# A recommendation tower: gathered groups turned by VectorE out of one table, 16-bit ids, single waits for pairs of tiles, and the first layer in parts

## The chip, the cores and the metric

One core of a Trainium2 chip runs the whole kernel in one launch. The time is device microseconds of that core, a median over several executions. The core has TensorE (PE, matrix products into PSUM), VectorE (DVE), ScalarE (ACT), GpSimd (POOL, here used to issue gathers) and SyncE (SP, here used to issue the direct DMAs). A kernel's engines run their own instruction lists in order, and meet at semaphores.

## The reference

```python
# ids (512, 40) int32; tbl_f (1000 to 125000 rows, 32) float32
e = jnp.stack([tbl_0[ids[:, 0]], ..., tbl_39[ids[:, 39]]], axis=1)     # (512, 40, 32)
iidx, jidx = jnp.triu_indices(40, k=1)                                 # 780 pairs
z = jnp.einsum('bpd,pde,bpe->bp', e[:, iidx], bilinear_matrices, e[:, jidx])
h = jnp.concatenate([z, dense_ctx], axis=1)                            # (512, 796)
h = jnp.maximum(h @ W_top1 + b_top1, 0.0)                              # (512, 512)
h = jnp.maximum(h @ W_top2 + b_top2, 0.0)                              # (512, 256)
y = h @ W_top3                                                         # (512, 1)
```

For each of 780 pairs of fields, one embedding row is multiplied by a 32x32 matrix and then by the other field's row, for each of the 512 samples; the 780 numbers and 16 dense inputs go through three layers.

## The kernel before, in words

**Groups.** The 40 fields form 10 groups of 4. A group's embeddings stand in `xt[:, t, :]` as 128 rows (4 fields times 32) by 512 samples, in float32. There are two ways to fill a group.

- Four groups (positions 0, 1, 3 and 5, `HOT_POS`) hold small tables and are picked by matrix product. VectorE compares the ids of the group, broadcast to all partitions, with a row number ("hot" steps, L320), and TensorE multiplies the 0/1 result by the table in three bfloat16 pieces (L385). The pieces `rest` and `low` come from VectorE too (L330, L332). 8, 8, 10 and 10 such rounds make 36 rounds. Ids are int32; ScalarE turns them to float16 (`narrow_ids`, L271), and all rounds but the first two compare the float16 ids.
- Six groups (`GATHER_POS`) are gathered row by row by 96 indirect DMAs that GpSimd issues (L217), 16 a group, each of 128 rows of one field's table. TensorE transposes four 128x128 tiles into `t_ps` (a "turn" step, L396), and ScalarE copies them to `xt` (L289).

**Units.** A unit (t, u), u up to t, covers all pairs of groups t and u; there are 55, in the order (0,0), (1,0), (1,1), (2,0) and so on. For each of the 4 fields of u (3 where u = t, called a diagonal unit here) TensorE makes one tile of `y_ps` with a 32-row matmul (L423); the trace shows two instructions per matmul. VectorE multiplies pairs of tiles by `xt[:, t, :]` into `prod` (L345, two instructions a unit, half 2k and half 2k+1 for unit k), and TensorE adds up over the 32 embedding rows with a selecting matrix into `z_ps` (a "sum" step, L446). Every 8 units ScalarE copies `z_ps` to a block of `z_t` (L294). There are 7 blocks.

**Buffers.** `y_ps` has 3 slots of 2 banks, so a half uses the slot of the half three before it. Before unit k TensorE waits once, for half 2k-2 to be read, which is more than its first pair of tiles needs. `z_ps` and `t_ps` have a bank each; `t_ps` is shared by rounds, turns and first-layer steps.

**Order.** It is written by hand: `schedule()` makes one list for TensorE and ScalarE: unit k, sum k-1, then whatever `AFTER` puts behind unit k. `vector_schedule()` makes VectorE's list: the rounds of `AFTER` come ahead of the unit of that number. Of the 36 rounds 11 come ahead of unit 0 and 5 around it, the rest are spread up to unit 13.

**Layers.** The first layer takes 4 parts of 128 outputs by 7 blocks. Blocks 0 to 3 are four steps of 4 matmuls, after units 34, 36, 38 and 42 (L405). Blocks 4 and 5 come at the end, after sums 53 and 54 (`late_blocks`, L369), block 6 after that (L454), VectorE adds the two halves (L351), and then layer two (L460) and three (L469) follow.

**Loads.** SP issues in order: ids, broadcast ids and table of pick group 0, of 1, matrices, tables of 2 and 3, more matrices, dense inputs; then the ids of groups 2 and 3, each behind a wait for earlier rounds; then the remaining matrices and weights. ScalarE's queue issues the row numbers, the identity (`eye`) and the selecting matrix.

Of the kernel before, what the change touches and what calls it, by code (L numbers as in the profile page):

```python
# [9 lines left out]
F16 = mybir.dt.float16  # L10
# [22 lines left out]

HOT_POS = [0, 1, 3, 5]
# [4 lines left out]
GATHER_POS = [t for t in range(GROUPS) if t not in HOT_POS]  # L39

# [42 lines left out]
def schedule():  # L83
# [3 lines left out]
    for k in range(-1, UNITS + LAG):  # L87
# [7 lines left out]
        for what in ("turn", "hot", "l1"):  # L95
            steps += [(what, n) for n, after in enumerate(AFTER[what]) if after == k]
# [13 lines left out]
def fills_bank(what, k):  # L110

    return what in ("turn", "l1") or (what == "hot" and ROUND[k][1] == HOT_ROWS[ROUND[k][0]] - 1)


def bass_dlrm_tower(nc, ids, hot_ids, numbers, hot_tables, tables, dense, mats, w1, b1, w2, b2, w3, ident, select, dense_sel, out):
    steps = schedule()
    fills = [s for s in steps if fills_bank(*s)]

    def fills_to(what, k):

        return fills.index((what, k)) + 1
# [422 lines left out]
```

## Time and profile before

| | us |
|---|---|
| median of 3 runs | 220.88 (219.36 to 221.36) |
| the profiled execution | 218.29 |
| its span, first to last instruction | 216.5 |
| TensorE busy | 182.4 |
| VectorE busy | 162.2 |
| GpSimd busy | 98.1 |
| ScalarE busy | 25.7 |
| granted TensorE clock, mean | 0.997 of full |

The span is from the first to the last instruction of the profiled execution; its own time is 1.8 us more. Busy times of engines overlap, so they don't add up to the span; matmuls are pipelined, and their ends are modelled, so the distance between the starts of two things is a safer measure than the length of one. In the chain of waits each line is a piece of the one path that ended last.

### The profile page before, as it was taken

Reading aid. Unit: us, or ns where it says so; the run is one execution under the profiler, and the core shown is the slowest. Engines: PE = TensorE matmul, PEld = TensorE weight load, DVE = VectorE, ACT = ScalarE, POOL = GpSimd, SP = SyncE. Lnnn points to the kernel's source line nnn. Section 1 sums busy time; section 2 is a strip of 40 time slices with the busy share of each in tenths; the row PEclk is TensorE's granted clock in tenths of the full one; section 3 lists DMA queues with packets and bytes.
Section 4 is the critical chain, followed back from the end, with each engine's and each line's share of the span. In section 5 each row is a group of like instructions: output and inputs, shape, how many; then the busy total and the mean of one; then the engine's idle time right before and its main releaser. Section 6 shows DMA issues by size and latency. Waiting matters only on the chain.

```text
span 216.5 us, 3263 instructions
## 1 busy us (share of the span) xinstructions
PE 182.4 (84%) x1392; PEld 55.0 (25%) x1392; DVE 162.2 (75%) x158; ACT 25.7 (12%) x33; POOL 98.1 (45%) x100
## 2 busy tenths in 40 slices
PE   0097694998599998899988899999998899999993
PEld 0032121332133221221212222322222121233433
DVE  0699869998999989989989993473957898960500
ACT  2331223002010021010100101011201010001411
POOL 4787777777877777777777770000000000000000
PEclk9999999999999999999999999999999999999998
DMA  6998079920000100100010000000000000000000
GB/s 227 372 401 283 12 292 421 402 58 12 12 15 11 16 12 12 17 13 12 14 16 12 14 13 3 5 0 0 3 0 0 0 3 0 0 3 0 0 0 0
DMA packets 7950, 14.55 MB, mean 67 GB/s; under 512 B 2784, under 2 KB 6000, under 8 KB 7296
## 3 DMA queue, kind: packets, MB, share of 16 engines
q1 hardware_dynamic: 4432, 12.65, 15.2%
q0 software_dynamic: 3072, 1.58, 4.3%
q8 instruction: 11, 0.18, 0.3%
q10 hardware_dynamic: 432, 0.12, 0.2%
q14 instruction: 3, 0.02, 0.0%
HBM read 14.33 MB, written 0.00 MB: 66 GB/s over the span
## 4 chain that ended last, share of the span: by engine, by line
PE 54%; DVE 32%; issue 7%; DMA 3%; ACT 1%; SPq 0%; DVEq 0%
DVE prod L345 26%; PE y_ps L423 23%; PE z_ps L446 7%; PE t_ps L385 7%; PE t_ps L405 7%; PE y_ps L369 3%; DVE hot L320 3%; PE y_ps L460 3%; DMA table<-hot_tables 3%; DVE rest L330 2%; PE y_ps L454 2%; DVE low L332 1%; PE t_ps L396 1%; PE t_ps L469 1%; ACT xt L289 1%
## 5 line engine op out<-in xcount | busy, mean ns | idle before, releaser
L345 DVE TENSOR_TENSOR prod<-y_ps,xt 128x1024 f32<-128x1024 f32 x110 | 124.1, 1170 | 26.6 <-PE y_ps L423 19.3
L217 POOL DMA_INDIRECT x_rows<-tbl,ids_sb x96 | 97.9, 1019 | 31.6 <-issue 29.0
L423 PE MATMUL y_ps<-xt,m_sb 32*128 32x512 f32 x420 | 62.6, 639 | 11.0 <-DVE prod L345 10.8
L446 PE MATMUL z_ps<-prod,sel 128*32 128x512 f32 x420 | 58.5, 604 | 0.2
L385 PE MATMUL t_ps<-hot,table 128*32 128x512 bf16 x144 | 15.9, 403 | 19.2 <-DVE low L332 17.3
L320 DVE TENSOR_SCALAR hot<-hot_id,number 128x2048 bf16<-128x2048 f16 (+1 forms) x36 | 26.8, 788 | 6.2 <-DMA hot_id<-hot_ids 6.2
L423 PEld LDWEIGHTS y_ps<-xt,m_sb 32*128 32x128 f32 x420 | 17.5, 183 | 49.8 <-DVE prod L345 32.1
L446 PEld LDWEIGHTS z_ps<-prod,sel 128*32 128x32 f32 x420 | 8.7, 107 | 43.6 <-DVE prod L345 34.0
L385 PE MATMUL t_ps<-hot,low 128*32 128x512 bf16 x144 | 15.6, 393 | 0.0
L385 PE MATMUL t_ps<-hot,rest 128*32 128x512 bf16 x144 | 15.6, 393 | 0.0
L405 PE MATMUL t_ps<-z_t,w_sb 128*128 128x512 f32 x32 | 14.8, 605 | 0.0
L289 ACT ACTIVATE xt<-t_ps 128x512 f32<-128x512 f32 x10 | 6.0, 595 | 69.4 <-PE t_ps L385 39.9
L385 PEld LDWEIGHTS t_ps<-hot,table 128*32 128x32 bf16 x144 | 4.3, 96 | 31.3 <-DVE low L332 19.6
L294 ACT ACTIVATE z_t<-z_ps 128x512 f32<-128x512 f32 x7 | 4.2, 597 | 62.2 <-PE z_ps L446 62.2
L351 DVE TENSOR_TENSOR hot_id<-y_ps,hot_id 128x512 f32<-128x512 f32 x4 | 2.8, 692 | 8.8 <-PE y_ps L454 8.8
L271 ACT ACTIVATE hot_id<-hot_id 128x2048 f16<-128x2048 int32 x4 | 7.6, 1910 | 11.7 <-DMA hot_id<-hot_ids 11.7
L405 PEld LDWEIGHTS t_ps<-z_t,w_sb 128*128 128x128 f32 x32 | 5.7, 189 | 9.1 <-issue 9.1
L369 PE MATMUL y_ps<-z_t,w_sb 128*128 128x512 f32 x16 | 7.4, 606 | 0.0
L460 PE MATMUL y_ps<-hot_id,w_sb 128*128 128x512 f32 x16 | 7.0, 592 | 0.0
L286 ACT ACTIVATE hot_id<-t_ps,b_sb 128x512 f32<-128x512 f32 x4 | 2.7, 687 | 30.6 <-PE t_ps L405 30.6
L330 DVE TENSOR_TENSOR rest<-table 128x1024 f32<-128x1024 f32 (+1 forms) x4 | 5.4, 1350 | 1.0 <-DMA table<-hot_tables 1.0
L332 DVE TENSOR_TENSOR low<-rest 128x1024 bf16<-128x1024 f32 (+1 forms) x4 | 5.4, 1358 | 0.1
(20 smaller groups left out, 37.2 us busy)
## 6 DMA issues: line engine op xcount, KB each, us to landing
hot_id<-hot_ids SPq DMA_DIRECT2D x4, 1024.0 KB, 4.9
w_sb<-w SPq DMA_DIRECT2D x1, 1792.0 KB, 13.9
x_rows<-tbl,ids_sb POOLq DMA_INDIRECT x96, 2.4
table<-hot_tables SPq DMA_DIRECT2D x2, 640.0 KB, 10.5
table<-hot_tables SPq DMA_DIRECT2D x2, 512.0 KB, 6.8
m_sb<-mats SPq DMA_DIRECT2D x1, 640.0 KB, 9.0
m_sb<-mats SPq DMA_DIRECT2D x1, 576.0 KB, 7.7
m_sb<-mats SPq DMA_DIRECT2D x1, 512.0 KB, 6.8
```

What stands on the lines that cost most here:

```text
L217: pool.indirect_dma_start(out=x_rows[:, g, bt, f, :], out_offset=None, in_=tables[field], in_offset=row).then_inc(gathered[g], 16)
L271: nc.scalar.activation(hot_id16[:, o % ID_RING, :], hot_id[:, o % ID_RING, :], ACT.Copy).then_inc(hot_id16_done, 1)
L289: nc.scalar.activation(xt[:, t, :], t_ps[:], ACT.Copy).then_inc(t_out, 1)
L320: nc.vector.tensor_scalar(hot[:, k % HOT_RING, :, :].rearrange("p f b -> p (f b)"), ids_of[:, o % ID_RING, :], number[:, o, r:r + 1], None ...
L330: nc.vector.tensor_tensor(left, whole, upper(whole), ALU.subtract).then_inc(rest_done, 1)
L345: nc.vector.tensor_tensor(prod[:, k % PROD_UNITS, 2 * half:2 * half + w, :], y_ps[:, 2 * slot:2 * slot + w, :], xt[:, t, :].unsqueeze(1).t ...
L369: nc.tensor.matmul(y_ps[:, LATE_BANK[m], :], w1_sb[:, b, m * P:(m + 1) * P], z_t[:, b, :], start=(b == EARLY_BLOCKS), stop=False, skip_gro ...
L385: last = nc.tensor.matmul(t_ps[f * DIM:(f + 1) * DIM, :], pieces[piece][:, f, :], hot[:, k % HOT_RING, f, :], start=(r == 0 and piece == 0 ...
L405: last = nc.tensor.matmul(t_ps[:], w1_sb[:, b, m * P:(m + 1) * P], z_t[:, b, :], start=(b == 0), stop=(b == EARLY_BLOCKS - 1))
L423: last = nc.tensor.matmul(y_ps[:, 2 * slot + s % 2, :], m_sb[rows, k, :], xt[rows, u, :], start=True, stop=True)
L446: last = nc.tensor.matmul(z_ps[s * DIM:(s + 1) * DIM, :], window, prod[:, k % PROD_UNITS, s, :], start=starts, stop=(k >= last_unit(b) - 1 ...
L460: last = nc.tensor.matmul(y_ps[:, L2_BANK[c], :], w2_sb[:, m, c * P:(c + 1) * P], h1[:, m, :], start=(m == 0), stop=(m == M1 - 1), skip_gr ...
```

## The change

- Gathered groups: the host puts all tables of gathered fields into one array `rows` and gives, beside the ids, the first row of each field's table. GpSimd adds the two (one instruction), and gathers 32 samples of 4 fields at a time (partition 32s+i is field s, sample i of the chunk), again 96 indirect DMAs of 128 rows. VectorE transposes the group in 32x32 blocks straight into `xt` (`nc.vector.transpose`, 128x512), ahead of the first unit of the group. TensorE's transposes, the identity and ScalarE's copies for these groups are gone.
- Ids for comparing are the lower 16-bit halves (int16), for all four groups with a place of their own, so that SP waits for nothing and ScalarE converts nothing; all 36 rounds compare int16.
- TensorE waits ahead of each pair of tiles for the slot of that pair alone; sums lag by two units in place of one, with 4 places in `prod` in place of 3.
- All 16 rounds of the first two groups come ahead of unit 0; the other rounds move too.
- First layer: blocks 0 to 2 and 3 to 4 are parts. They are 20 steps of one matmul, one after most units from 26 to 37 and 42 to 49; VectorE adds part two to part one ("join", 4 instructions). At the end block 5 alone is left of the late blocks.
- The order of SP's loads: matrices 0 to 2, then ids and tables of group 2, matrices 3, dense, then ids and tables of group 3.

```diff
-PROD_UNITS = 3
-LAG = 1
+PROD_UNITS = 4
+LAG = 2
-EARLY_BLOCKS = 4
+PARTS = [(0, 3), (3, 5)]
+LATE_BLOCK = 5
+L1_STEP = [(i, m, b) for i in range(len(PARTS)) for m in range(M1) for b in range(*PARTS[i])]
 AFTER = {
-    "turn": [1, 6, 14, 20, 30, 40],
-    "hot": [-1] * 8 + [-1, -1, -1, 0, 0, 0, 0, 0] + [2, 2, 2, 3, 3, 3, 4, 4, 5, 5]
-    + [7, 7, 8, 8, 9, 9, 10, 11, 12, 13],
-    "l1": [34, 36, 38, 42],
+    "hot": [-1, -1, -1, -1, -1, -1, -1, -1, -1, -1, -1, -1, -1, -1, -1, -1, 0, 1, 1, 1, 1, 2, 2, 3, 3, 3, 7, 7, 8, 8,
+        9, 9, 10, 11, 12, 13],
+    "l1": [26, 27, 28, 29, 30, 31, 32, 33, 34, 35, 36, 37, 42, 44, 45, 46, 47, 47, 48, 49],
+    "turn": [3, 10, 21, 28, 36, 45],
 }
...
 def vector_schedule():
+    early = [j for j, after in enumerate(AFTER["hot"]) if after < 0]
+    steps = [("hot", j) for j in early]
+    for k in range(UNITS):
+        steps += [("turn", g) for g, before in enumerate(AFTER["turn"]) if before == k]
+        if k == 0:
+            first = [("hot", j) for j, after in enumerate(AFTER["hot"]) if after == 0]
+            steps += first[:1] + [("unit", 0)] + first[1:]
+            continue
         steps += [("hot", j) for j, after in enumerate(AFTER["hot"]) if after == k]
         steps.append(("unit", k))
+        steps += [("join", L1_STEP[n][1]) for n, after in enumerate(AFTER["l1"]) if after == k
+                  and L1_STEP[n][0] == 1 and L1_STEP[n][2] == PARTS[1][1] - 1]
...
# GpSimd
-            pool.wait_ge(ids_in, 16)
-            for g, t in enumerate(GATHER_POS):
-                for f in range(G):
-                    field = FIELD[t][f]
-                    for bt in range(BT):
-                        row = bass.IndirectOffsetOnAxis(ap=ids_sb[:, bt, field:field + 1], axis=0)
-                        pool.indirect_dma_start(out=x_rows[:, g, bt, f, :], out_offset=None,
-                                                in_=tables[field], in_offset=row).then_inc(gathered[g], 16)
+            pool.wait_ge(ids_in, 32)
+            nc.gpsimd.tensor_tensor(row[:], ids_sb[:], first_row[:], ALU.add).then_inc(row_done, 1)
+            pool.wait_ge(row_done, 1)
+            for g in range(GATHERS):
+                for c in range(CHUNKS):
+                    n = g * CHUNKS + c
+                    pool.indirect_dma_start(out=x_rows[:, g, c, :], out_offset=None, in_=rows,
+                                            in_offset=bass.IndirectOffsetOnAxis(ap=row[:, n:n + 1], axis=0)
+                                            ).then_inc(gathered[g], 16)
...
# ScalarE's queue
-            act.dma_start(eye[:], ident).then_inc(eye_in, 16)
+            act.dma_start(first_row[:], first_rows).then_inc(ids_in, 16)
...
# VectorE
                     nc.vector.tensor_scalar(hot[:, k % HOT_RING, :, :].rearrange("p f b -> p (f b)"),
-                                            ids_of[:, o % ID_RING, :], number[:, o, r:r + 1], None,
+                                            hot_id[:, o, :], number[:, o, r:r + 1], None,
                                             ALU.is_equal).then_inc(hot_done, 1)
...
+                if what == "turn":
+                    t = GATHER_POS[k]
+                    dve.wait_ge(gathered[k], 16 * CHUNKS)
+                    nc.vector.transpose(xt[:, t, :], x_rows[:, k, :, :].rearrange("p c d -> p (c d)")).then_inc(turned, 1)
+                if what == "join":
+                    dve.wait_ge(part_done, M1 + k + 1)
+                    nc.vector.tensor_tensor(h1[:, k, :], t_ps[:], h1[:, k, :], ALU.add).then_inc(joined, 1)
...
# TensorE
                 if what == "l1":
+                    i, m, b = L1_STEP[k]
+                    first, end = PARTS[i]
...
+                    if b == first:
+                        bank_free(pe, "l1", k + end - first - 1)
+                    pe.wait_ge(z_out, b + 1)
+                    last = nc.tensor.matmul(t_ps[:], w1_sb[:, b, m * P:(m + 1) * P], z_t[:, b, :],
+                                            start=(b == first), stop=(b == end - 1), skip_group_check=True)
...
                 if what == "unit":
-                    if k >= 2:
-                        pe.wait_ge(prod_done, 2 * k - 1)
-                    elif k == 1:
-                        pe.wait_ge(prod_done, 1)
                     for s in range(tiles_in(k)):
-                        slot = (2 * k + s // 2) % Y_SLOTS
+                        half = 2 * k + s // 2
+                        slot = half % Y_SLOTS
+                        if s % 2 == 0 and half >= Y_SLOTS:
+                            pe.wait_ge(prod_done, half - Y_SLOTS + 1)
```

## Rows read from the trace of the kernel before

**Rows 1.** Page of the profile, busy time by engine, and GB/s in 40 slices of 5.4 us.

```profile
PE 182.4 (84%) x1392; PEld 55.0 (25%) x1392; DVE 162.2 (75%) x158; ACT 25.7 (12%) x33; POOL 98.1 (45%) x100
...
GB/s 227 372 401 283 12 292 421 402 58 12 12 15 11 16 12 12 17 13 12 14 16 12 14 13 3 5 0 0 3 0 0 0 3 0 0 3 0 0 0 0
```

**Rows 2.** Chain of waits, 100 to 104 us: start, length (us), what.

```profile
99.36 1.15 PE y_ps L423 x8
...
100.53 1.24 DVE prod L345
...
101.81 1.15 PE y_ps L423 x8
```

**Rows 3.** Chain of waits, whole span: two rounds, a first-layer block, a sum, a unit.

```profile
43.90 1.30 PE t_ps L385 x24
...
129.03 3.63 PE t_ps L405 x8
...
179.50 1.00 PE z_ps L446 x8
180.50 1.08 PE y_ps L423 x8
```

**Rows 4.** VectorE in order of time, 78 to 130 us: start, length, [idle before].

```profile
80.55 12.17 DVE L345 TENSOR_TENSOR prod<-y_ps,xt 128x1024 f32<-128x1024 f32 x10 [0.89 <-ACT xt L289]
...
95.62 14.63 DVE L345 TENSOR_TENSOR prod<-y_ps,xt 128x1024 f32<-128x1024 f32 x12 [0.89 <-ACT xt L289]
```

**Rows 5.** Chain of waits, 189 to 217 us.

```profile
192.47 3.63 PE y_ps L369 x8
...
204.15 6.87 PE y_ps L460 x16
```

**Rows 6.** VectorE in order of time, first 50 us.

```profile
16.70 1.21 DVE L330 TENSOR_TENSOR rest<-table 128x1024 f32<-128x1024 f32 x1
...
19.09 2.17 DVE L320 TENSOR_SCALAR hot<-hot_id,number 128x2048 bf16<-128x2048 f16 x3
...
32.14 1.48 DVE L330 TENSOR_TENSOR rest<-table 128x1280 f32<-128x1280 f32 x1
...
35.06 1.42 DVE L320 TENSOR_SCALAR hot<-hot_id,number 128x2048 bf16<-128x2048 f16 x2
36.40 1.80 DVE L345 TENSOR_TENSOR prod<-y_ps,xt 128x1024 f32<-128x1024 f32 x2
38.13 2.25 DVE L320 TENSOR_SCALAR hot<-hot_id,number 128x2048 bf16<-128x2048 f16 x3
...
43.88 2.34 DVE L345 TENSOR_TENSOR prod<-y_ps,xt 128x1024 f32<-128x1024 f32 x2
46.15 1.40 DVE L320 TENSOR_SCALAR hot<-hot_id,number 128x2048 bf16<-128x2048 f16 x2
```

**Rows 7.** Groups of instructions by form: busy us, mean ns, idle before.

```profile
L320 DVE TENSOR_SCALAR hot<-hot_id,number 128x2048 bf16<-128x2048 f16 x34 | 24.3, 759 | 0.0
...
L345 DVE TENSOR_TENSOR prod<-y_ps,xt 128x512 f32<-128x512 f32 x10 | 6.8, 680 | 0.0
...
L320 DVE TENSOR_SCALAR hot<-hot_id,number 128x2048 bf16<-128x2048 int32 x2 | 2.6, 1283 | 6.2 <-DMA hot_id<-hot_ids 6.2
```

**Rows 8.** All engines in order of time, first 9 us.

```profile
6.16 1.29 DVE L320 TENSOR_SCALAR hot<-hot_id,number 128x2048 bf16<-128x2048 int32 x1 [6.16 <-DMA hot_id<-hot_ids]
...
8.45 1.22 DVE L330 TENSOR_TENSOR rest<-table 128x1024 f32<-128x1024 f32 x1 [1.01 <-DMA table<-hot_tables]
```

**Rows 9.** DMA issues, KB each, us to landing.

```profile
x_rows<-tbl,ids_sb POOLq DMA_INDIRECT x96, 2.4
...
eye<-ident ACTq DMA_DIRECT2D x1, 64.0 KB, 5.1
```

**Rows 10.** Gathers on GpSimd: all 96 by tile, ns min/median/max.

```profile
L217 POOL DMA_INDIRECT x_rows<-tbl,ids_sb x96: 940/944/1859, 3.1 to 128.9; - x96
```

**Rows 11.** Gathers on GpSimd, 3 to 50 us, by line.

```profile
L217 POOL DMA_INDIRECT x_rows<-tbl,ids_sb x35 | 37.4, 1070 | 13.0 <-issue 10.4 <-DMA ids_sb<-ids 2.6
```

More of the change, by code:

```diff
@@ L9 @@
 I32 = mybir.dt.int32
-F16 = mybir.dt.float16
+I16 = mybir.dt.int16
 BF16 = mybir.dt.bfloat16
@@ L94, in schedule @@
                 steps.append(("z", b))
-        for what in ("turn", "hot", "l1"):
+        for what in ("hot", "l1"):
             steps += [(what, n) for n, after in enumerate(AFTER[what]) if after == k]
@@ new lines, in vector_schedule, with picked, ends_bank, bass_dlrm_tower @@
+    return steps
+def picked(o):
+    return sum(HOT_ROWS[:o + 1]) - 1
+def ends_bank(what, k):
+    if what == "l1":
+        return L1_STEP[k][2] == PARTS[L1_STEP[k][0]][1] - 1
+    return what == "hot" and k in [picked(o) for o in range(HOTS)]
+def bass_dlrm_tower(nc, ids, first_rows, rows, hot_ids, numbers, hot_tables, dense, mats, w1, b1, w2, b2, w3, select, dense_sel, out):
+    steps = schedule()
+    fills = [s for s in steps if ends_bank(*s)]
+    def read_by_vector(what, k):
+        return what == "l1" and L1_STEP[k][0] == 1
+    def bank_free(engine, what, k):
+        before = fills[:fills.index((what, k))]
+        if before and read_by_vector(*before[-1]):
+            engine.wait_ge(joined, len([s for s in before if read_by_vector(*s)]))
+        elif before:
+            engine.wait_ge(t_out, len([s for s in before if not read_by_vector(*s)]))
+    def x_there(engine, t):
@@ L504 @@
         select[p, SEL_COLS + p // DIM] = 1.0
-    ids = a["ids"].reshape(P, BT, FIELDS)
+    ids = np.ascontiguousarray(a["ids"].reshape(P, BT, FIELDS).transpose(1, 0, 2).reshape(BATCH, FIELDS))
+    lower = ids.view(np.int16).reshape(BATCH, FIELDS, 2)[:, :, 0]
+    gather_fields = [f for t in GATHER_POS for f in FIELD[t]]
+    by_chunk = ids[:, gather_fields].reshape(CHUNKS, DIM, GATHERS, G)
+    sizes = [len(a[f"tbl_{f}"]) for f in gather_fields]
+    starts = np.array([sum(sizes[:n]) for n in range(len(sizes))], np.int32).reshape(GATHERS, G)
+    first_rows = np.broadcast_to(starts.T[:, None, :, None], (G, DIM, GATHERS, CHUNKS))
     hot_fields = [f for p in HOT_POS for f in FIELD[p]]
@@ L518 @@
     arrays = {
-        "ids": ids,
-        "hot_ids": ids[:, :, hot_fields].transpose(2, 1, 0).reshape(HOTS, G * BATCH),
+        "ids": by_chunk.transpose(3, 1, 2, 0).reshape(P, GATHERS * CHUNKS),
+        "first_rows": first_rows.reshape(P, GATHERS * CHUNKS),
+        "rows": np.concatenate([a[f"tbl_{f}"] for f in gather_fields]),
+        "hot_ids": lower[:, hot_fields].T.reshape(HOTS, G * BATCH),
         "numbers": numbers,
@@ L529 @@
         "w3": a["W_top3"].reshape(M2, P).T,
-        "ident": np.eye(P, dtype=np.float32),
         "select": select,
@@ L533 @@
     }
-    arrays |= {f"tbl_{f}": a[f"tbl_{f}"] for t in GATHER_POS for f in FIELD[t]}
     arrays = {k: np.ascontiguousarray(v) for k, v in arrays.items()}
```

137 lines of the change are left out of this document (45 added, 92 removed).

## The prediction

> **What bounds the kernel now.** The busy times come first [rows 1]: TensorE 182 and VectorE 162 of a span of 216.5 us. Neither is full, so the two must wait for each other, and the chain of waits shows how. In a quiet stretch it alternates: a unit's tiles on TensorE (1.15 us), a product on VectorE (1.24), the next unit's tiles [rows 2]. One lap is 101.81 - 99.36 = 2.45 us a unit. Neither engine needs that long. VectorE's two products run 46.15 - 43.88 = 2.27 from start to start when nothing holds them, a diagonal unit's 38.13 - 36.40 = 1.73 [rows 6]. TensorE's sum takes 1.00 and a unit's tiles 1.07 where they follow each other (tiles begin at 180.50 and are a modelled 1.08 long) [rows 3], together 2.07. So the lap is the one wait ahead of a unit: all its tiles start only when half 2k-2 is read, and end just as VectorE runs out. Anything that TensorE does besides then stops VectorE: the first-layer blocks of 3.63 us [rows 3], and the turns with ScalarE's copy, 0.89 us of idle VectorE each [rows 4]. From about 190 us the chain is TensorE's alone [rows 5].
>
> **Start.** The first table lands at 8.45 and the picks start behind its pieces [rows 8]. Ahead of that table 80 KB of ids, 1,024 KB of broadcast ids and the 512 KB of the table itself go out; after, 48, 512 and 512. At 227 to 372 GB/s [rows 1] the 544 KB less are 1.5 to 2.4 us, and what shares the queues takes part of it: I take 1.55, range 0.5 to 2.5.
>
> **Prices that no row shows.** (a) A compare of int16. Nearest rows: float16, as wide, 0.759 us, and int32, twice as wide, 1.283 [rows 7]. I take the float16 price by width, and 0.67 from start to start (36.40 less 35.06, for two [rows 6]). The Trainium skill's "VectorE: DVE Perf Modes", section "What auto-detection actually checks", names 16-bit elements, not floats, as the condition of the fast modes, which speaks for the same value; no run here shows an int16. (b) A 32x32-block transpose, 128x512 float32. The product of the same size takes 0.680 [rows 7]; a 128x2048 int32 compare bounds it above at 1.28. I take 0.65; each 0.3 more costs 1.8 in six. (c) A join is the same size, 0.68. (d) A lone first-layer matmul. Eight instructions take 3.63 between other work, but 16 in a run of their kind 6.87, 0.43 each [rows 3, 5]: so going over to that shape and back costs 3.63 - 8 x 0.43 = 0.20. A step of one matmul (two instructions) is then 0.86 + 0.20 = 1.06; 0.86 is its floor, and 1.5 a ceiling with the edge three times as dear.
>
> **Up to unit 15, VectorE bound.** The pieces of pick group 1 start at 16.70 [rows 6], after at 15.15 (the rounds ahead of them are the same). From there VectorE has to do: pieces 2.39 (16.70 to 19.09) and 2 x 2.92 (32.14 to 35.06) [rows 6] = 8.2; 27 compares x 0.67 = 18.1; 10 full and 5 diagonal units 22.7 + 8.7; two transposes 1.3. Sum 59.0. TensorE has 2.07 + 1.30 [rows 3] = 3.4 us for a unit with two rounds, VectorE 2.27 + 1.34 = 3.6, so TensorE lags nowhere. Unit 15 starts at 74.1; before at 80.55 [rows 4]. Gain 6.4, of which 1.55 from the start.
>
> **Units 15 to 26.** The waits for single pairs break the lap: half h needs half h-3 read, so two pairs may be in work while VectorE reads the third, and TensorE's 2.07 is hidden under 2.27. 11 full units 25.0, diagonal 1.7, a transpose 0.65: 27.4, unit 26 ends at 101.5. Before: 95.62 + 14.63 = 110.25 [rows 4]. The gain is now 8.8.
>
> **Units 27 to 54, TensorE bound.** Here twenty lone matmuls come in. From the end of unit 26's tiles (a product pair ahead, 101.5 - 2.3 = 99.2) to the start of sum 53 TensorE does 28 units x 1.07 = 30.0, 29 sums 29.0, the dense inputs' eight instructions 1.0, as a sum's [rows 3], 20 steps x 0.86 + 19 edges x 0.20 = 21.0: 81.0. With 0.5 for units 38 to 41, where it waits for VectorE again, sum 53 starts at 180.7. VectorE has only 64.7 (24 x 2.27 + 3 x 1.73 + 3 x 0.65 + 4 x 0.68) in this stretch and idles for some 15: joins and the last three transposes lie in that idle time. Were TensorE faster, they would count. Before, sum 53 ends where the first late block starts, 192.47, so starts at 191.47 [rows 5]. Gain 10.8: of the 8.8 and what the looser waits and the absent turns give, the four matmuls that block 4 moves in here (3.4) and the edges (15 more x 0.20) take a part back.
>
> **Tail.** Four of eight late matmuls are gone, 8 x 0.43 = 3.4 [rows 5]. The joins are done long before the tail, and the rest of it is as before. ScalarE's lost conversions and copies cost nothing before, but for the 0.89 behind turns.
>
> **Sum.** 10.8 + 3.4 = 14.2, span 216.5 to 202.3, the profiled execution's 218.29 to 204.1. The median shown is 220.88, 2.6 above that execution; against it 206.7. I say 206.
>
> **Gathers.** GpSimd is free of the path while its groups land in time. It starts at 3.1 [rows 10]; after, it also needs the first rows, on ScalarE's queue in the place of `eye`, which took 5.1 from its issue at 1.2 [rows 9], and adds them: say 7. At 1.07 + 0.30 = 1.37 a gather while compares run [rows 11] group 0 is in at 7 + 16 x 1.37 + 2.4 [rows 9] = 31, needed at 36; group 1 at 53, needed at 60; at 1.25 later, group 3 at 93 for 104, group 5 at 133 for some 150. A gather of 1.86 [rows 10] shows that it can be held. The Trainium skill's "SBUF — State Buffer", section "Who interferes with whom", says that VectorE in its two-port modes and GpSimd lock each other out; here the trace agrees (1,070 ns in the first 50 us against a median of 944). By it, sixteen compares in one go would hold the gathers harder than before; 16 gathers at 1.86 + 0.30 would make group 0 4 to 6 us late, paid once, since GpSimd has slack later.
>
> **Rivals.**
> - *The compare is not fast on int16* (slower than before). Its place is VectorE ahead of unit 13. At the int32 price it adds 0.52 x 36 = 18.9, about 2 of it hidden in the first eight rounds: 206 + 17 = 223. It decides from 1.17 us a compare (14.2 over 36 on top of 0.76 and the hidden part). At one element a cycle, read from the products (1024 elements in 1.14 us [rows 6], so 2.28), it would be near 260. For: no row has an int16. Against: the step from 1.28 to 0.76 came with width alone as far as rows tell. 6 in 100.
> - *Pairs run one after the other.* The four tiles of a unit overlap (eight instructions in 1.07). If a wait between them kept the second pair from joining the first, a unit would cost up to 1.0 more; TensorE would then bound from unit 15 on, 12 x 0.8 + 28 x 1.0 = 37 at worst, 243; half of it gives 224. Against: in the TensorE-bound stretch the wait is long met. 5 in 100, two of them ending as no change.
> - *Late gathers, dear transposes or edges:* group 0 late by 5, transposes at 1.28 (half hidden, 2), edges at 0.4 (3.8): 209 to 217. 14 in 100.
> - *More comes in than summed:* edges hidden by loading weights early (3.8), start 2.5: 199. 7 in 100.
> - *The change does little*, as the freed time turns into waits at hand-overs that the sums of durations can't show: 0.3 us at each of 40 units is 12, so 218.5. 5 in 100.
>
> **How the numbers follow.** The forecast as summed has 63 in 100, with 201 to 212 as its own range (start 1, edges 3, medians 1.5). Adding the dearer cases up to 214 and the better ones from 199 leaves 2 in 10 out. About 1%, 2.2 us, is what a measurement of this kernel can tell. Faster by over 1%: 63 + 13 + 7 + some = 0.85. Within: 0.07, from the last rival, part of the pairs. Slower: the two mechanisms, 0.08.
>
> **What would show it.** Compares at 0.74 to 0.78; VectorE's full units 2.27 apart between 15 and 26 with no idle; unit 15 at 74; from unit 27 TensorE without gaps and VectorE idle by 15; tiles, sum and lone matmul 3.1 a unit; sum 53 at 181; two late blocks of 1.9 in place of 3.6. Wrong if compares are near 1.3, if tiles take 2 us a unit, or if VectorE waits for a gather.

## The result, and the profile after

The changed kernel takes 208.1 us (median of 4 runs, 207.73 to 208.88), the kernel before 220.12 (4 runs, 219.22 to 221.36). The ratio is 0.9455, 95% interval 0.9392 to 0.9518, so the change saves 12 us. The forecast was 206 with a range of 199 to 214. The profiled execution took 208.05, its span 206.0 where the sum had 202.3. The 3.7 between the two are what this section looks for.

The page of the changed kernel comes first: busy time by engine, GB/s in slices of 5.2 us, and the chain by engine. It answers to [rows 1].

```profile
PE 186.4 (90%) x1368; PEld 58.0 (28%) x1368; DVE 165.7 (80%) x168; ACT 14.7 (7%) x23; POOL 97.7 (47%) x101
...
GB/s 109 358 402 402 419 397 42 13 16 16 12 14 13 13 13 13 13 18 14 13 16 13 13 13 13 17 5 0 0 5 0 0 0 3 0 0 0 0 0 0
...
PE 84%; DVE 10%; DMA 4%; issue 1%; SPq 0%; ACT 0%; DVEq 0%
```

TensorE is busy 4 us longer than before and 90% of the span. ScalarE lost 11 us of work. The first slice moves 109 GB/s, before 227 [rows 1].

The forms of VectorE's instructions give the prices that no row of before had (busy us, mean ns, idle before), beside [rows 7].

```profile
L325 DVE TENSOR_SCALAR hot<-hot_id,number 128x2048 bf16<-128x2048 int16 x36 | 25.8, 761 | 8.0 <-DMA hot_id<-hot_ids 7.5 <-PE t_ps L391 0.5
...
L342 DVE STREAM_TRANSPOSE xt<-x_rows 128x512 f32<-128x512 f32 x6 | 4.2, 699 | 0.0
```

The int16 compare is as fast as the float16 one (761 against 759 ns). The transpose takes 699 ns by itself and 0.63 from start to start.

VectorE in order of time, first 10 us and then 38 to 110 us, answers to [rows 4], [rows 6] and [rows 8]. The columns are start, length, instruction, count and idle time before.

```profile
9.04 1.22 DVE L335 TENSOR_TENSOR rest<-table 128x1024 f32<-128x1024 f32 x1 [0.81 <-DMA table<-hot_tables]
...
38.10 0.70 DVE L342 STREAM_TRANSPOSE xt<-x_rows 128x512 f32<-128x512 f32 x1
...
47.60 2.36 DVE L357 TENSOR_TENSOR prod<-y_ps,xt 128x1024 f32<-128x1024 f32 x2 [0.47 <-issue]
...
78.00 13.13 DVE L357 TENSOR_TENSOR prod<-y_ps,xt 128x1024 f32<-128x1024 f32 x12 [0.47 <-issue]
91.05 0.70 DVE L342 STREAM_TRANSPOSE xt<-x_rows 128x512 f32<-128x512 f32 x1
91.78 13.66 DVE L357 TENSOR_TENSOR prod<-y_ps,xt 128x1024 f32<-128x1024 f32 x12
106.39 1.82 DVE L357 TENSOR_TENSOR prod<-y_ps,xt 128x1024 f32<-128x1024 f32 x2 [0.94 <-PE y_ps L421]
```

The pieces of the first table start at 9.04, not at 6.9. Transpose 0 at 38.10 waits for no gather. Unit 15's first product is at 78.00 (80.55 before). From there twelve units and a transpose run with no idle, to 91.78 + 13.66 = 105.44. Then VectorE waits 0.94 before unit 27 and 0.71 to 0.77 before each of the units 28 to 38; later stretches without such gaps (units 39 to 42, for one) come between others that have them.

The chain of waits of the changed kernel, by start and length in us, shows the two regimes and the tail. It answers to [rows 2], [rows 3] and [rows 5].

```profile
99.71 1.26 PE y_ps L421 x8
100.97 1.00 PE z_ps L444 x8
...
125.08 1.00 PE z_ps L444 x8
126.08 1.06 PE t_ps L403 x2
127.13 1.07 PE y_ps L421 x8
...
185.06 1.85 PE z_ps L444 x16
186.92 1.91 PE y_ps L375 x4
...
189.82 1.92 PE y_ps L375 x4
```

Up to 103 us a lap is tiles 1.26 and sum 1.00, together 2.26, which is VectorE's 2.27. Tiles take 1.07 when nothing holds them, so the 1.26 contain 0.19 of waiting, though the chain calls all of it TensorE. From unit 27 on a lap that holds a lone first-layer matmul is sum, matmul, tiles: 3.12 from start to start, and in such a lap TensorE never stops. Two late blocks of 1.9 stand where two of 3.63 stood [rows 5]: of each, half the matmuls are gone.

All 10.5 us of span are accounted for by four landmarks:

| stretch | before | after | saved |
|---|---|---|---|
| start to unit 15's first product | 80.55 | 78.00 | 2.55 |
| from there to the end of unit 26's products | 29.70 | 27.44 | 2.26 |
| from there to VectorE's first addition in the tail | 91.37 | 87.19 | 4.18 |
| from there to the end of the span | 14.88 | 13.37 | 1.51 |

The last row is the landing of the 2 KB result, 2.9 us before and 1.4 after; the work ahead of it, up to ScalarE's last copy, takes the same 11.36 us. "Unit 15 to the tail" below means rows two and three together: **before 121.07, after 114.63**.

### The profile page after: what moved, and what is told of

It is laid out like the page before. It is cut to its first block, busy times and chain, and to the rows that moved or that the text cites. A ratio compares the mean times of both kernels' runs of the same rounds, so it can differ in the third digit from the quotient of the medians.

```text
span 206.0 us, 3187 instructions
## 1 busy us (share of the span) xinstructions
PE 186.4 (90%) x1368; PEld 58.0 (28%) x1368; DVE 165.7 (80%) x168; ACT 14.7 (7%) x23; POOL 97.7 (47%) x101
## 4 chain that ended last, share of the span: by engine, by line
PE 84%; DVE 10%; DMA 4%; issue 1%; SPq 0%; ACT 0%; DVEq 0%
PE y_ps L421 31%; PE z_ps L444 25%; PE t_ps L403 10%; PE t_ps L391 9%; DVE hot L325 4%; DMA table<-hot_tables 4%; PE y_ps L458 3%; DVE low L337 3%; DVE rest L335 3%; PE y_ps L375 2%; PE y_ps L452 2%; PE t_ps L467 1%; DVE prod L357 1%; PE z_ps L436 0%; SPq L254 0%
## 5 line engine op out<-in xcount | busy, mean ns | idle before, releaser
L357 DVE TENSOR_TENSOR prod<-y_ps,xt 128x1024 f32<-128x1024 f32 x110 | 122.2, 1166 | 13.8 <-PE y_ps L421 11.3
L244 POOL DMA_INDIRECT x_rows<-rows,row x96 | 96.7, 1007 | 29.2 <-issue 29.0
L421 PE MATMUL y_ps<-xt,m_sb 32*128 32x512 f32 x420 | 71.0, 649 | 0.0
L421 PEld LDWEIGHTS y_ps<-xt,m_sb 32*128 32x128 f32 x420 | 24.2, 185 | 40.5 <-issue 29.2
L325 DVE TENSOR_SCALAR hot<-hot_id,number 128x2048 bf16<-128x2048 int16 x36 | 25.8, 761 | 8.0 <-DMA hot_id<-hot_ids 7.5
L403 PE MATMUL t_ps<-z_t,w_sb 128*128 128x512 f32 x40 | 22.2, 642 | 0.0
L363 DVE TENSOR_TENSOR h<-y_ps,h 128x512 f32<-128x512 f32 x4 | 2.8, 692 | 6.4 <-PE y_ps L452 6.4
L458 PE MATMUL y_ps<-h,w_sb 128*128 128x512 f32 x16 | 7.0, 592 | 0.0
L295 ACT ACTIVATE xt<-t_ps 128x512 f32<-128x512 f32 x4 | 2.4, 597 | 50.0 <-PE t_ps L391 50.0
L391 PEld LDWEIGHTS t_ps<-hot,low 128*32 128x32 bf16 x144 | 4.4, 103 | 4.4 <-issue 1.1
L391 PEld LDWEIGHTS t_ps<-hot,rest 128*32 128x32 bf16 x144 | 4.3, 101 | 2.5 <-issue 1.0
```

What stands on the lines that cost most here:

```text
L244: pool.indirect_dma_start(out=x_rows[:, g, c, :], out_offset=None, in_=rows, in_offset=bass.IndirectOffsetOnAxis(ap=row[:, n:n + 1], axis= ...
L325: nc.vector.tensor_scalar(hot[:, k % HOT_RING, :, :].rearrange("p f b -> p (f b)"), hot_id[:, o, :], number[:, o, r:r + 1], None, ALU.is_e ...
L357: nc.vector.tensor_tensor(prod[:, k % PROD_UNITS, 2 * half:2 * half + w, :], y_ps[:, 2 * slot:2 * slot + w, :], xt[:, t, :].unsqueeze(1).t ...
L391: last = nc.tensor.matmul(t_ps[f * DIM:(f + 1) * DIM, :], pieces[piece][:, f, :], hot[:, k % HOT_RING, f, :], start=(r == 0 and piece == 0 ...
L403: last = nc.tensor.matmul(t_ps[:], w1_sb[:, b, m * P:(m + 1) * P], z_t[:, b, :], start=(b == first), stop=(b == end - 1), skip_group_check ...
L421: last = nc.tensor.matmul(y_ps[:, 2 * slot + s % 2, :], m_sb[rows, k, :], xt[rows, u, :], start=True, stop=True)
```

## The experiments

In the first eight runs TensorE issued hardly a matmul for some 110 us within the first rounds, in the kernel before as well (its medians there are 329.8 and 329.6). So their whole times (medians of 325.2 to 329.7; two executions of run 2 took 460.6 and 1064.4) decide nothing, and stretches behind this hold are compared; what it looks like stands at the end. From unit 15 on the granted clock is 1.00 in all these traces. Ahead of unit 15 it is not: in runs 1 to 5 and 8 it stands at 0.50 for 3.4 us between the starts of units 6 and 8, and in run 3 also from the hold up to 150.7. The changed kernel itself was not run beside them. That such a stretch can be trusted is shown by the kernels that change only what lies ahead of it: 114.63 and 114.64 in runs 5 and 6, with the hold, and 114.65 and 114.64 in runs 9 and 12, without. The 3.4 us at 0.50 can be trusted to cost little too: from unit 1 to unit 15 runs 2, 4 and 5, which have them, took 44.90 to 45.02, and runs 6 and 7, which don't, 44.71 and 45.05.

The theory under test was the prediction's: VectorE bounds up to unit 26, TensorE after it, and the pair waits are what lets VectorE run through. The rival was that TensorE bounds from early on, as the chain of waits says (84% PE).

**1. Transposes twice, groups 0 to 2.** Added to the changed kernel; the extra copy is not used.

```diff
+                    if k < 3:
+                        nc.vector.transpose(h2[:, 0, :], x_rows[:, k, :, :].rearrange("p c d -> p (c d)"))
```

> The changed kernel with the first three transposes done twice (the spare one goes to a place that is not yet in use), 0.7 us of VectorE each, ahead of units 3, 10 and 21. Theory: VectorE bounds up to unit 26, so the time grows by what VectorE gets, 3 x 0.63 = 1.9 us, span 206.0 to 207.9. Rival, read from the chain of waits of the changed kernel (TensorE 84%): TensorE bounds all along, and the three cost nothing, span 206.0. A little less than 1.9 where a transpose falls into a gap at a diagonal unit: 1.3 to 1.9.

Measured: two of the extra transposes, ahead of unit 15, made the stretch from unit 1 to unit 15 46.04 us, where the changed kernel's first trace has 45.22 and runs 2 and 4 to 7 have 44.71 to 45.05: 0.8 to 1.3 more. The third, inside the units 15 to 26, made unit 15 to the tail 115.24, 0.61 longer. At 0.63 for each, VectorE's work ahead of unit 27 is paid in full, as far as this spread lets it be told. "TensorE bounds all along" fell.

**2. The same for groups 3 to 5**, behind unit 26.

> The changed kernel with the last three transposes done twice, ahead of units 28, 36 and 45. Theory: TensorE bounds from unit 27 on and VectorE idles 0.77 us a unit, so 3 x 0.63 us more on VectorE cost nothing or up to 0.5 in all, span 206.0 to 206.5. Rival, that VectorE's added work is still on the path in this stretch: 1.9 more, 207.9.

VectorE in order of time, around the first doubled transpose:

```profile
227.28 0.70 DVE L343 STREAM_TRANSPOSE h<-x_rows 128x512 f32<-128x512 f32 x1
227.91 0.67 DVE L344 STREAM_TRANSPOSE xt<-x_rows 128x512 f32<-128x512 f32 x1
228.72 2.36 DVE L359 TENSOR_TENSOR prod<-y_ps,xt 128x1024 f32<-128x1024 f32 x2
```

The gap after them (228.58 to 228.72) is 0.14, where the single transpose left 0.73. Three extra transposes of 0.63 are 1.9 us of VectorE, and unit 15 to the tail grew by 0.20, to 114.83. Behind unit 26 they lie in VectorE's idle time.

**3. One wait a unit again**, in the changed kernel.

```diff
+                    if k >= 1:
+                        pe.wait_ge(prod_done, max(1, 2 * k - 1))
...
-                        if s % 2 == 0 and half >= Y_SLOTS:
-                            pe.wait_ge(prod_done, half - Y_SLOTS + 1)
```

> The changed kernel with the one wait ahead of a unit of before (for half 2k-2) in place of one ahead of each pair. Theory: units 15 to 26 go back to a lap of 2.45 from 2.27 and lose about 0.8 behind each diagonal unit: 12 x 0.18 + 1 to 2 = 3 to 4 us by unit 26; in the TensorE-bound stretch VectorE still idles and the wait is long met, under 1 us; the early part 1 us; together 3.5 to 6, span 209.5 to 212. Rival, that the longer lag of sums and the absent turns made the lap shorter, not the waits: 0 to 1 us, span 206 to 207.

VectorE in order of time in units 15 to 26, and the chain of waits in the same stretch:

```profile
189.26 12.18 DVE L357 TENSOR_TENSOR prod<-y_ps,xt 128x1024 f32<-128x1024 f32 x10 [0.77 <-issue]
...
204.21 14.63 DVE L357 TENSOR_TENSOR prod<-y_ps,xt 128x1024 f32<-128x1024 f32 x12 [0.15 <-DVE xt L342]
```

```profile
193.00 1.15 PE y_ps L420 x8
...
194.18 1.24 DVE prod L357
...
195.46 1.15 PE y_ps L420 x8
```

Ten products take 12.18 and twelve 14.63, in laps of 2.45; the alternation of [rows 2] is back. The sums still lag by two units here, so the longer lag is not what shortened the lap. Unit 15 to the tail took 117.78 (+3.15).

Ahead of unit 15 the clock disturbs the comparison. VectorE's longest stop there, and the busy times in the six microseconds ahead of it (the third number from the end is the granted clock):

```profile
153.31 2.36 DVE L357 TENSOR_TENSOR prod<-y_ps,xt 128x1024 f32<-128x1024 f32 x2 [2.25 <-PE y_ps L420]
```

```profile
144.00:150.00 6.00, 5.13 (x28) 1.28 (x31) 5.60 (x8) 0.00 (x0) 0.00 (x0) 0.50 0.01 3
```

Unit 2 to unit 15 took 44.86, against 41.12 to 41.63 in the changed kernel and runs 5 and 6. But of the 3.2 to 3.7 more, 2.2 to 2.3 lie between unit 2 and unit 4 (8.91 against 6.57 to 6.68), while TensorE ran at a granted 0.50: in the chain a unit's tiles take 2.09 and a sum 1.86 there. What the unit-wide wait costs in this piece can't be told from it. From unit 4 to unit 15 it took 35.95 against 34.55 to 34.96, 1.0 to 1.4 more. So what the run shows of the wait alone is 3.15 + 1.0 to 1.4, 4.1 to 4.6 us, inside the 3.5 to 6 that had been expected.

**4. First-layer matmuls in groups of three and two.**

```diff
-    "l1": [26, 27, 28, 29, 30, 31, 32, 33, 34, 35, 36, 37, 42, 44, 45, 46, 47, 47, 48, 49],
+    "l1": [27, 27, 27, 30, 30, 30, 33, 33, 33, 36, 36, 36, 43, 43, 45, 45, 47, 47, 49, 49],
```

> The changed kernel with its 20 first-layer steps in 8 groups (three in a row behind units 27, 30, 33 and 36, two behind 43, 45, 47 and 49) in place of 19 separate ones. Theory: a switch to that matmul shape and back costs 0.20 us, TensorE bounds here, so 11 fewer switches give 2.2 us, span 206.0 to 203.8. Rival: groups of 2.8 us stop VectorE for longer than its buffers cover and it then bounds the units between them; the gain is used up, span 206 to 208.

```profile
230.91 6.88 DVE L357 TENSOR_TENSOR prod<-y_ps,xt 128x1024 f32<-128x1024 f32 x6 [2.63 <-issue]
240.45 6.88 DVE L357 TENSOR_TENSOR prod<-y_ps,xt 128x1024 f32<-128x1024 f32 x6 [2.66 <-PE y_ps L421]
```

This is VectorE in order of time. Fewer changes of shape save TensorE time, yet unit 15 to the tail took 115.60, 0.97 more and not 2.2 less. A group stops VectorE for 2.66, and between groups the units run at VectorE's 2.27 and not at TensorE's 2.07. The theory behind this run (the edges of 0.20 are a saving to be had) fell, and the rival held.

**5. Every partition reads its own copy of the ids** (4 KB rows, the same bytes moved).

```diff
-                sp.dma_start(hot_id[:, o, :], hot_ids[o:o + 1, :].to_broadcast([P, G * BATCH])
+                sp.dma_start(hot_id[:, o, :], hot_ids[o]
...
-        "hot_ids": lower[:, hot_fields].T.reshape(HOTS, G * BATCH),
+        "hot_ids": np.repeat(lower[:, hot_fields].T.reshape(HOTS, 1, G * BATCH), P, axis=1),
```

> The changed kernel with the 16-bit ids laid out once per partition in HBM, so that each partition reads its own 4 KB and not all the same 4 KB; bytes moved are the same. Theory: the one shared source of 4 KB is what slows the first loads (about 0.45 us for a 4 KB packet, where an 8 KB packet of before took 0.33), so the first table lands near 6.9 in place of 9.0, and the span falls by about 2 us to 204. Rival: the number of packets and the other loads in flight set the time, and the table lands at 9.0 plus or minus 0.3, span 206.

The DMA queue that loads ids, tables and matrices, in the microsecond from 3 to 4 (packets, MB, share of 16 engines), for the kernel before, the changed one and this one, and below them VectorE's first instructions of this run:

```profile
q1 hardware_dynamic: 44, 0.36, 91.6%
```

```profile
q1 hardware_dynamic: 26, 0.11, 73.3%
```

```profile
q1 hardware_dynamic: 64, 0.26, 74.0%
```

```profile
7.18 1.23 DVE L335 TENSOR_TENSOR rest<-table 128x1024 f32<-128x1024 f32 x1 [0.81 <-DMA table<-hot_tables]
```

The share by the packets gives the time of one: before 0.916 x 16 / 44 = 0.33 us for 8 KB, changed 0.733 x 16 / 26 = 0.45 us for 4 KB, own rows 0.740 x 16 / 64 = 0.18 us. With rows of its own the first table's pieces start at 7.18, 1.9 earlier than in the changed kernel's first trace, and 1.5 to 2.3 earlier than in all eight traces here that load like it (8.65 to 9.47). By the same sum the packets of 4 KB in these eight traces take 0.34 to 0.50 us each, never less than the 0.33 of 8 KB. So the half-width ids did halve the bytes, and reading the same 4 KB from all partitions gave the time back.

**6. The first table ahead of the first ids**, and its pieces ahead of the first compares.

```diff
-            load_hot_ids(0)
             load_tables(0)
+            load_hot_ids(0)
```

> The changed kernel with the first table loaded ahead of the first ids, and VectorE making that table's pieces ahead of the first compare. Theory: the table's 512 KB land after 3 to 4.5 us, the pieces end near 7.5, the ids land by 7 to 8.5, the first round starts at 8.5 to 9.5 in place of 11.6: span 203 to 204.5. Rival: the ids, now second, land as late as the table did (9.0), the first compare ends at 9.8 and rounds start then: 1.7 less, but rounds run at the slow start of TensorE anyway, span 204.5 to 206.

VectorE's first instruction in this run:

```profile
5.71 1.22 DVE L323 TENSOR_TENSOR rest<-table 128x1024 f32<-128x1024 f32 x1 [5.71 <-DMA table<-hot_tables]
```

The pieces start at 5.71 and the first round at 9.01, against 9.04 and 11.57. The whole run took 325.87, 0.9883 of the kernel before (0.9814 to 0.9951), which the hold makes hard to read. Unit 15 to the tail was 114.64.

**7. The first layer as before**: blocks of four matmuls, no joins, four late blocks.

```diff
-PARTS = [(0, 3), (3, 5)]
-LATE_BLOCK = 5
+PARTS = [(0, 4)]
+LATE_BLOCK = 4
...
-    "l1": [26, 27, 28, 29, 30, 31, 32, 33, 34, 35, 36, 37, 42, 44, 45, 46, 47, 47, 48, 49],
+    "l1": [34] * 4 + [36] * 4 + [38] * 4 + [42] * 4,
```

> The changed kernel with the first layer as before the change: blocks 0 to 3 in four groups of 4 behind units 34, 36, 38 and 42, blocks 4 and 5 in the tail, no joins. Theory: while TensorE bounds, moving block 4 out of the tail moves 3.4 us and saves none; what the parts gain is only that TensorE's spare time between units is used (about 0.2 us a unit over 18 units, 3.6), and they pay 15 switches of 0.20 (3.0). So the span stays within 1.5 us of 206.0, 205 to 208. Rival, that block 4's 3.4 us in the tail are a saving of their own: span 209.4 or more.

```profile
245.00 1.82 DVE L357 TENSOR_TENSOR prod<-y_ps,xt 128x1024 f32<-128x1024 f32 x2 [3.52 <-PE y_ps L421]
...
253.14 4.62 DVE L357 TENSOR_TENSOR prod<-y_ps,xt 128x1024 f32<-128x1024 f32 x4 [3.31 <-PE y_ps L421]
261.28 9.14 DVE L357 TENSOR_TENSOR prod<-y_ps,xt 128x1024 f32<-128x1024 f32 x8 [3.52 <-PE y_ps L421]
```

Again VectorE in order of time: three of the four stops cost it 3.52, the other 3.31. Unit 15 to the tail took 115.43, 0.80 more. That is what "first layer in parts" brings in the changed kernel. The 3.4 saved in the tail are nearly all paid where block 4 went.

**8. The kernel before with pair waits alone.**

```diff
-                    if k >= 2:
-                        pe.wait_ge(prod_done, 2 * k - 1)
-                    elif k == 1:
-                        pe.wait_ge(prod_done, 1)
...
-                        slot = (2 * k + s // 2) % Y_SLOTS
+                        half = 2 * k + s // 2
+                        slot = half % Y_SLOTS
+                        if s % 2 == 0 and half >= Y_SLOTS:
+                            pe.wait_ge(prod_done, half - Y_SLOTS + 1)
```

> The kernel before with nothing changed but the waits: one ahead of each pair of tiles. Theory: units lap at 2.27 in place of 2.45 where nothing else is in the way, about 28 of them, and the waits behind diagonal units shrink from 0.8 to about 0.3: 5 + 3 = 8 us, less where the first-layer groups bound anyway, so 5 to 8, span 216.5 to 208.5 to 211.5. Rival: with sums lagging by one unit TensorE must wait for the second product of a unit before it can go on, and gains at most 2 us, span 214.5 or more.

```profile
208.46 15.60 DVE L345 TENSOR_TENSOR prod<-y_ps,xt 128x1024 f32<-128x1024 f32 x14 [1.08 <-ACT xt L289]
```

VectorE runs 14 products in 15.60, a lap of 2.27 instead of 2.45, but still stops 1.10 and 1.08 for ScalarE's copies at the turns ahead of units 15 and 21. Unit 15 to the tail went from 121.07 to 116.97, 4.10 of the 6.44 that the whole change gains there. Ahead of unit 15 it gained 0.1 (from unit 2 on 44.06 against 44.15), where run 3 lost at least 1.0 to 1.4. That the pair waits help there only once the turns through TensorE and ScalarE are gone would fit both, but was not tested. The result lies between theory and rival. Beside run 7 it also prices the rest of the change behind unit 15: 116.97 less 115.43 is 1.5 us for all but the pair waits and the first layer in parts.

**9. The changed kernel again**, on the chip of runs 10 and 11, where no hold occurred.

> The changed kernel itself, as the base for the next two on the same chip. Expected: first table's pieces start at 8.6 to 9.5 us, and 114.6 us from unit 15's first product to VectorE's first addition in the tail, as in its first trace; span 206.0 where TensorE is not held in the first rounds.

208.68 us (207.38 to 209.4), 0.9481 of the kernel before (0.9416 to 0.9546). The stretch from 50 to 60 us of its trace shows a granted clock of 0.66, which the changed kernel's first trace does not have; unit 15 came at 79.31. Unit 15 to the tail took 114.65.

**10. First-layer matmuls in pairs**, 16 of them, from unit 19 on, and no fifth block.

```diff
-PARTS = [(0, 3), (3, 5)]
-LATE_BLOCK = 5
+PARTS = [(0, 2), (2, 4)]
+LATE_BLOCK = 4
...
-    "l1": [26, 27, 28, 29, 30, 31, 32, 33, 34, 35, 36, 37, 42, 44, 45, 46, 47, 47, 48, 49],
+    "l1": [19, 19, 22, 22, 25, 25, 28, 28, 34, 34, 37, 37, 40, 40, 43, 43],
```

> The changed kernel with blocks 0 to 3 of the first layer in 8 pairs of matmuls (blocks 0 and 1 behind units 19, 22, 25, 28, blocks 2 and 3 behind 34, 37, 40, 43) and blocks 4 and 5 in the tail. Theory, mended after groups of three and four had gained nothing: TensorE's total counts, matmuls, switches and the laps in which it waits for VectorE, wherever it stands. 11 switches fewer are 2.2 us, and units that carry none (24 of 39 in place of 20) wait 0.2 each, 0.8 back: 1.4 us less, range 0.5 to 2.5: from unit 15 to the tail's first addition plus what is moved into the tail. As 3.4 us are moved into the tail, the span counts: 1.4 below the changed kernel. Rival, that a pair still stops VectorE for longer than the three slots cover, and that this is lost: 0 to 1 us slower.

```profile
90.61 1.82 DVE L357 TENSOR_TENSOR prod<-y_ps,xt 128x1024 f32<-128x1024 f32 x2 [1.80 <-PE y_ps L421]
...
99.50 6.88 DVE L357 TENSOR_TENSOR prod<-y_ps,xt 128x1024 f32<-128x1024 f32 x6 [1.80 <-PE y_ps L421]
```

210.62 us (210.35 to 211.31), 1.9 above run 9; unit 15 to the tail 116.14 (+1.5). Each pair stops VectorE 1.80. The theory (1.4 less) fell, the rival held.

**11. Pairs, table first and own id rows together.**

> First-layer pairs as in the run before, and the first table ahead of the ids with its pieces made first, and the ids laid out once per partition. Theory: the table lands at 5.7 as it did ahead of the shared ids, the ids by 6 to 7, the first round starts at 9.0 or a little earlier in place of 11.5: 2.5 us less, and with the 1.4 of the pairs 3.9 below the changed kernel, span about 202. Rival, that an earlier start is lost again in the first rounds, where TensorE is slow and VectorE waits for it: 1.5 to 2.5 below.

208.89 us (208.03 to 210.31), 1.7 below run 10, with unit 15 at 75.81 instead of 77.40, though its first round began at 9.16 instead of 11.73. The 3.9 below the changed kernel that had been expected did not come: by the medians it is level with run 9.

**12. The changed kernel with table first and own id rows.**

> The changed kernel with only its start altered: first table ahead of the ids, its pieces made first, ids laid out once per partition; the first layer as in the change. Theory: the start gives here what it gave beside the pairs (e11 against e10: 1.6 us at unit 15, 1.7 in the median), and nothing behind unit 15 changes (114.6 us from unit 15 to the tail's first addition): median 206.4 against the 208.1 and 208.7 of the changed kernel, span 204.4. Rival, that the gain shrinks further because TensorE's slow first rounds simply begin earlier: 0 to 1 us.

TensorE in order of time in the first rounds, of the changed kernel and then of this one (start, length; each line is four matmuls of one product):

```profile
11.57 0.62 PE L391 MATMUL t_ps<-hot,table 128*32 128x512 bf16 x4 [11.57 <-DVE low L337]
11.97 0.65 PE L391 MATMUL t_ps<-hot,rest 128*32 128x512 bf16 x4
...
14.96 0.47 PE L391 MATMUL t_ps<-hot,low 128*32 128x512 bf16 x4
15.25 0.39 PE L391 MATMUL t_ps<-hot,table 128*32 128x512 bf16 x4
```

```profile
9.08 0.62 PE L395 MATMUL t_ps<-hot,table 128*32 128x512 bf16 x4 [9.08 <-DVE hot L338]
9.46 0.67 PE L395 MATMUL t_ps<-hot,rest 128*32 128x512 bf16 x4
...
14.15 0.47 PE L395 MATMUL t_ps<-hot,table 128*32 128x512 bf16 x4
14.44 0.40 PE L395 MATMUL t_ps<-hot,rest 128*32 128x512 bf16 x4
```

The first round starts 2.5 earlier (9.08 against 11.57), but every group of four then takes 0.43 from start to start until 14.2, and only then 0.22. In the changed kernel the fast pace begins at 15.0. Both show a granted clock of 1.00 in these stretches. Unit 15 comes at 76.75, 1.25 earlier than in the changed kernel's first trace, and the last compute instruction starts at 202.76 instead of 204.00. In this trace the result then landed after 2.8 us and not 1.4, and the span is 206.2. The median is 208.15 (207.81 to 209.8, 6 runs), 0.954 of the kernel before (0.9483 to 0.9598). That cannot be told from the changed kernel's 208.1 and 208.68. No version here is shown to beat the change.

## Why the prediction was right, and where it was off

The median was forecast at 206 and came at 208.1, the mechanism as argued, but the gain was put too high: 14.2 of span by the sum, 10.5 measured. By its own steps:

- **The start (failed).** It assumed that half the bytes take half the time: pieces at 6.9. They start at 9.04, later than before (8.45). Run 5 shows the cause for 1.5 to 2.3 us, by the trace that one compares with: 128 partitions that read the same 4 KB get 0.45 us a packet. This is the largest error, 2.1, still 2.4 at the second group's pieces (17.59 for 15.15), and the 1.55 that the sum had for it came out as a loss of 0.6.
- **Up to unit 15.** Predicted 59.0 of VectorE from the second pieces on; measured 78.00 - 17.59 = 60.4. Two gaps of 0.47 (at 47.60 and 78.00, each behind a diagonal unit) are 0.9 of the 1.4; the likely reason, not tested, is that such a unit's second product, of a single tile, is over too soon for the next tiles. So the gain here was 2.55 and not 6.4.
- **Units 15 to 26.** 27.4 predicted, 27.44 measured. Runs 3 and 8 show that it hangs on the pair waits.
- **Units 27 to 54.** From the end of unit 26's tiles (103.24) to the start of sum 53 (some 186.0, the second of the two sums at 185.06) 82.7, predicted 81.5. The lone matmul cost 1.06 as worked out. The 1.2 too few are laps in which VectorE bounds again (in the whole chain eight units' tiles take 1.26 to 1.45 there and not 1.07, in units 39 to 42, 44 and 52 to 54): 2.1 in all, where 0.5 was put. VectorE idles 13.8 from 105.44 to the end of unit 54's products, where some 15 was said; the 64.7 of work beside it adds up to 64.3 by the prediction's own terms.
- **Tail.** 3.4 predicted. From the start of the first late block to ScalarE's last copy it was 212.98 - 192.47 = 20.51 and is 204.00 - 186.92 = 17.08: 3.43 less. But run 7 puts its worth into place: the four matmuls of block 4 mostly moved, and parts and tail together bring 0.80.
- **Not in the sum:** the result's landing, 1.5 faster in this trace. It is 1.4 in run 9 too, and in runs 1 to 4, 6 and 7, but 2.6 to 3.1 in runs 5 and 10 to 12, and 2.9 and 2.7 in the kernel before and run 8. Both traces of the changed kernel have 1.4, so it can't be put down to chance from one execution to the next; why the kernels differ was not found, nor whether the change has a part in it. 3.9 (unit 15) + 1.2 - 1.5 make 3.6 of the 3.7. So the shorter landing hid 1.5 us of the error of the sum in this trace.
- **Prices.** Compare 761 ns (taken 759), join 686 (680), transpose 0.63 (0.65). The int16 compare is in this respect like float16 and unlike int32 (1,283 ns [rows 7]). The Trainium skill's "VectorE: DVE Perf Modes", section "What auto-detection actually checks", asks for 16-bit elements in its fastest mode and says nothing of floats; the trace agrees.
- **Gathers.** GpSimd began at 8.75 and not at 7: the first rows landed at 7.20 by its wait, and the addition took 0.83 and 0.28. No group was late: VectorE's six transposes have no idle before them. The 31 up to 50 us take 0.94 to 1.49 us each, median 1.02: held a little, never to the 1.86 that would have made group 0 late by 4 to 6. The Trainium skill's "SBUF — State Buffer", section "Who interferes with whom", lets VectorE's fast modes and GpSimd lock each other out; by that the trace shows at most a mild case.
- **Rivals.** Slow compares, pairs in sequence and late gathers are excluded by the rows above. Hand-over waits of 0.3 a unit did not come; two gaps of 0.47 did. The 206 itself was put 0.7 below its own sum of 206.7, with no reason given.

One sentence of the prediction misleads, though its number was right: that edges cost 3.8 and could be hidden. Runs 4, 7 and 10 show that grouping saves nothing. A unit that carries n first-layer matmuls costs TensorE 2.07 + 0.20 + 0.86 n, and a unit without any still costs VectorE 2.27. The edge fits exactly into TensorE's slack, so a lone matmul delays VectorE by some 0.8 (3.12 less 2.27 is 0.85, measured gaps 0.71 to 0.77), and one of a pair by 1.80 / 2 = 0.90, of three by 2.66 / 3 = 0.89, of four by 3.52 / 4 = 0.88. Being spread also puts transposes and joins into the gaps. "Too few edges counted" would not have raised the gain.

Where the 10.5 us of span between the two traces come from, as far as the runs divide them: 6.44 lie between unit 15 and the tail, of which the pair waits are 4.1 (run 8), the first layer in parts 0.8 (run 7), and the rest of the change, turns off TensorE and ScalarE among it, 1.5. Another 2.55 lie ahead of unit 15; taking the pair waits out costs 1.0 to 1.4 there (run 3), and putting them alone into the kernel before gains 0.1 (run 8). The landing is 1.5, not explained. So the pair waits are the largest part that a run shows. What the turns, the order of the rounds and the longer lag of sums have by themselves was not run.

## What to carry to other kernels

When two engines alternate and neither is full, add up each one's time per lap from start to start: if the lap is longer than both, look for one wait that covers more than the buffer needs, as this unit-wide wait did. Work inserted on one engine costs what exceeds the other's lap, so an edge that fits into slack is free, and here spreading such work beat grouping it. Price a load by its access pattern, not by its bytes alone, before booking a gain from narrower data.

## What the runs showed of the hardware

- **A shared source was slow, and no faster a packet when half as wide.** 0.45 us a packet for 128 readers of one 4 KB row (0.34 to 0.50 over eight traces), 0.33 for one 8 KB row, 0.18 for 4 KB rows of their own (115, 384 and 277 GB/s in that microsecond). Why was not tested.
- **The first rounds run at half pace, and the record of the clock does not show it.** Groups of four bf16 matmuls start every 0.43 us and later every 0.22, while the granted clock shows 1.00 throughout. In the changed kernel TensorE had done nothing before 11.57 and the pace rose at 15.0; in run 12 it had done nothing before 9.08 and rose at 14.2. The kernel before has it too, from 10.99 to 13.95. In run 1 the same groups start every 0.43 us from 133.76 to 136.32 at a granted 0.50: the pace of the first rounds is the one that the lower clock gives, though their record says 1.00. A start 2.5 earlier was worth 1.25.
- **A hold.** Busy time (count) of each engine, granted clock, DMA share and GB/s in stretches of run 1:

```profile
14.00:18.00 4.00, 3.73 (x44) 1.32 (x37) 1.49 (x2) 0.00 (x0) 3.03 (x4) 1.00 1.03 382
18.00:22.00 4.00, 1.70 (x12) 0.38 (x11) 0.75 (x1) 0.00 (x0) 3.15 (x3) 1.00 1.03 414
22.00:26.00 4.00, 3.07 (x11) 0.27 (x9) 0.00 (x0) 0.00 (x0) 2.91 (x4) 0.60 1.07 433
60.00:90.00 30.00, 0.00 (x0) 0.00 (x0) 0.99 (x1) 0.00 (x0) 22.73 (x24) 0.50 0.09 13
150.00:180.00 30.00, 26.63 (x250) 8.72 (x250) 29.49 (x34) 0.60 (x1) 0.00 (x0) 0.94 0.01 1
```

- Up to 17.3 us TensorE works as always, at 1.00. From 17.6 its matmuls come singly or a few at a time, with gaps that no wait explains, still at 1.00; only near 22.8 does the granted clock fall to 0.50 (1.2 GHz). After 45.8 it issues nothing for 87.6 us, and works again from 133.4, at 1.00 from 145.7 on but for 3.4 us near 178. So the fall of the clock comes after the work has thinned out and is not what began it; what did was not found. It came in both kernels on two chips and never on the third.
- **The same wait with and without a fall of the clock.** Ahead of the rounds of the last pick group TensorE waits 2.59 to 2.83 us for VectorE's pieces, in the changed kernel and in all runs but 8. The granted clock stays at 1.00 through it in the changed kernel's first trace and in runs 6, 7, 10 and 11, and falls to 0.50 in runs 1 to 5, 9 and 12. Run 9, the same view:

```profile
48.00:50.00 2.00, 2.00 (x19) 0.66 (x14) 2.00 (x3) 0.00 (x0) 1.70 (x2) 1.00 0.14 25
...
52.00:54.00 2.00, 0.39 (x4) 0.14 (x8) 1.97 (x3) 0.00 (x0) 1.70 (x2) 0.68 0.07 16
54.00:56.00 2.00, 2.00 (x24) 0.63 (x16) 2.00 (x3) 0.00 (x0) 1.39 (x3) 0.50 0.07 8
```

- In run 9 the clock is low from 52.7 to 59.6. Unit 7, which starts in it, still comes 0.2 earlier than in the changed kernel's first trace (54.13 for 54.34), unit 15 comes 1.3 later (79.31 for 78.00). In the other six it is low for 3.4 us, and costs nothing that shows: in run 12 the lead of 1.25 was there before the fall and after it. The changed kernel's first trace has such 3.4 us too, earlier, from 28.9 on (0.50 from 29 to 32), after TensorE had waited 1.69 us.
- **The last 2 KB** landed after 1.4 us in eight traces of the changed kernel and its variants and after 2.6 to 3.1 in four others, a difference larger than some of the effects measured here.
